# A decoder layer in one kernel: the cross attention's 24 middle steps written out in place of a loop of two, with constant addresses

## What is computed

```python
x = x + gated_slot_attention(layernorm(x))       # 4 heads, a recurrence over the 128 tokens
x = x + cross_attention(layernorm(x), ctx)       # 16 heads of 8
x = x + experts(layernorm(x))                    # 8 experts, top 2, LoRA pairs
```

```python
q = (query @ Wq.T + bq);  k = (key @ Wk.T + bk);  v = (value @ Wv.T + bv)     # heads of 8
scores = einsum(q, k) * 8 ** -0.5 + attn_mask
scores = where(pad, -inf, scores) + spatial_bias + directional_bias           # one array, twice
out = softmax(scores) @ v;  return out @ Wo.T + bo
```

## Time and profile before

| what | value |
|---|---|
| median of 3 runs | 597.54 us (595.57 to 598.49) |
| the profiled execution's own time | 593.18 us |
| its span in the profile | 591.4 us |
| slot attention, alone or in the lead | to about 217 us |
| cross attention, steps 4 to 27 (the loop) | about 242 to 418 us |
| experts | from about 432 us |
| mean granted TensorE clock | 0.987 of full speed |

### The profile page before, as it was taken

One profiled execution on the slowest core, in us unless ns is written; L12 is line 12 of the kernel. 1 busy time (PEld: TensorE's weight loads), 2 busy tenths in 40 slices (PEclk: granted clock), 3 DMA queues, 4 the chain that ended last, 5 costly groups with the idle time before them and its releaser, 6 DMA issues.

```text
span 591.4 us, 17340 instructions
## 1 busy us (share of the span) xinstructions
PE 530.9 (90%) x5328; PEld 408.2 (69%) x5328; DVE 481.9 (81%) x1945; ACT 398.3 (67%) x1033; POOL 355.5 (60%) x362
## 2 busy tenths in 40 slices
PE   4689999999997779999999999999976999999986
PEld 3467677777776547777777777777765778788865
DVE  2578888887877678999999999999988888888862
ACT  2668878878875378988999999999954333333321
POOL 6335555456445898888888888888824433333430
PEclk9899999999999989999999999999989999999999
DMA  6920000000000477888888888888600000000000
GB/s 159 241 37 2 1 1 1 0 0 0 1 1 2 81 130 130 154 154 150 153 153 150 153 151 152 150 154 152 104 2 2 1 19 19 18 18 18 19 18 19
DMA packets 84426, 42.44 MB, mean 72 GB/s; under 512 B 4378, under 2 KB 84132, under 8 KB 84388
## 3 DMA queue, kind: packets, MB, share of 16 engines
q1 hardware_dynamic: 83234, 41.63, 38.5%
q10 hardware_dynamic: 1154, 0.33, 0.2%
HBM read 39.86 MB, written 2.10 MB: 71 GB/s over the span
## 4 chain that ended last, share of the span: by engine, by line
PE 44%; DVE 22%; issue 19%; ACT 5%; POOL 5%; DVEq 1%; POOLq 0%; ACTq 0%
DVE c_P L1044 6%; PE banks L458 5%; PE banks L938 5%; PE banks L925 4%; PE banks L1246 4%; PE banks L891 3%; PE banks L1270 3%; DVE shared L723 3%; PE banks L914 2%; PE banks L449 2%; PE banks L422 2%; PE banks L904 2%; DVE banks L696 2%; DVE shared L702 2%; ACT c_P L972 2%
## 5 line engine op out<-in xcount | busy, mean ns | idle before, releaser
L1138 POOL TENSOR_TENSOR c_bias<-c_fside,c_cm 128x2048 f32<-128x2048 f32 x32 | 146.3, 4571 | 27.3 <-PE banks L891 24.6
L972 ACT ACTIVATE c_P<-c_P,c_min 128x128 f32<-128x128 f32 x512 | 156.6, 391 | 2.4 <-DVE c_min L1044 2.4
L1044 DVE CUSTOM_DVE_ANT_0 c_P<-banks,c_bias 128x128 f32<-128x128 f32 x512 | 116.3, 284 | 5.3 <-PE banks L891 2.3
L925 PE MATMUL banks<-ident,c_P 128*128 128x128 f32 x512 | 74.8, 279 | 6.6 <-DVE shared L1080 5.8
L925 PEld LDWEIGHTS banks<-ident,c_P 128*128 128x128 f32 x512 | 57.9, 142 | 32.9 <-issue 28.4
L1080 DVE COPY shared<-banks 128x512 f32<-128x512 f32 x96 | 65.6, 684 | 0.0
L1246 PE MATMUL banks<-um,lb_s 128*128 128x512 f32 x192 | 55.6, 404 | 2.7 <-ACT shared L1303 1.9
L1482 POOL TENSOR_TENSOR xs<-shared,xs 128x512 fp32r<-128x512 f32 x8 | 10.7, 1334 | 66.5 <-ACT xs L1313 66.5
L1303 ACT ACTIVATE shared<-banks,bi_col 128x512 f32<-128x512 f32 x32 | 22.0, 688 | 38.2 <-PE banks L1246 38.2
L1246 PEld LDWEIGHTS banks<-um,lb_s 128*128 128x128 f32 x192 | 34.2, 188 | 18.9 <-ACT shared L1303 12.5
L1044 DVE DVE_READ_ACCUMULATOR2_ANT c_min<- 128x1 f32 x512 | 42.5, 83 | 0.0
(11 more groups left out here) (195 smaller groups left out, 1295.3 us busy)
## 6 DMA issues: line engine op xcount, KB each, us to landing
c_fside<-in_fside_Bx16xSxS_dram SPq DMA_DIRECT2D x64, 512.0 KB, 7.2
c_ctx<-in_ctx_dram SPq DMA_DIRECT2D x32, 64.0 KB, 5.0
out_dram<-shared SPq DMA_DIRECT2D x8, 256.0 KB, 2.3
X<-in_x_dram SPq DMA_DIRECT2D x3, 512.0 KB, 5.5
kmask_sb<-in_mask_BxS_bf_dram SPq DMA_DIRECT2D x1, 512.0 KB, 7.4
X<-in_x_dram SPq DMA_DIRECT2D x2, 128.0 KB, 3.3
c_P<-in_L_ffn_wi_dram SPq DMA_DIRECT2D x1, 256.0 KB
c_P<-in_L_ffn_lora_B_dram SPq DMA_DIRECT2D x1, 256.0 KB
```

The source lines that it names most:

```text
L925: last = nc.tensor.transpose(bank(2 + i % 2)[:, 128 * j:128 * j + 128], P[:, q, XG * i + j, :], ident[:])
L972: last = nc.scalar.activation(P[:, par, h, :], P[:, par, h, :], ACT.Exp, bias=mn[:, par, h:h + 1], scale=-1.0)
L1044: last = nc.vector.tensor_tensor_reduce(out=P[:, o, h, :], in0=bank(score_banks(n + 1)[i])[:, 128 * j:128 * j + 128], in1=fm[:, o, h, :], ...
L1138: nc.gpsimd.tensor_tensor(fm[:, q, :, :], fs[:, q, :, :], bc(cm[:], XH), ALU.add).then_inc(C["fm"], 1)
```

## The change

The four engines no longer loop over steps 4 to 27: their code holds each of the 24 steps, made by the same function as the steps at both ends, so with constant addresses and constant counts in the waits. The operations, their order on each engine and their buffers are the same. SyncE's loop of loads stays, and so do the loops of the other two stages.

```diff
         def x_loop(engine, step):
-            with engine.Fori(2, B // 2 - 2, 1) as m:
-                step(m, 0, True, True, True, True, True)
-                step(m, 1, True, True, True, True, True)
+            for n in range(4, B - 4):
+                x_peeled(step, n)
```

## The result

The changed kernel takes 588.17 us in the median (586.12 to 590.89, 4 runs) against 597.46 us of before (595.57 to 598.49): a ratio of 0.9864 with a 95% interval of 0.9815 to 0.9913. Its profiled execution took 586.37 us, that of before 593.18, so 6.8 us less at the same mean granted clock of 0.987. The forecast was 590.3 by the medians and 586.0 by the profiled execution.

The account below looks back on a forecast made before the run. VectorE was taken to arrive last in the loop, ScalarE and TensorE together to bind written-out steps. Gains of 5.4, 1.6 and 0.2 us sum to 7.2, off the median 597.54: 590.3 us, 8-in-10 range 586.0 to 595.5.

Parts of the forecast that it names:

- The sum: Cross attention, steps 4 to 27: all 24 go to 7.04 us from a stretch of 176.17, gaining 7.2 us.
- The jump and the address work: VectorE arrives last in the loop; eleven steps with jumps back gain 5.4 us, twelve others 1.6, the first 0.2.
- gain nothing by themselves: TensorE, ScalarE and GpSimd: their register work and jumps hide under waits, so no gain of their own.
- VectorE at 6.94: VectorE's time between additions to the stream in written-out code, claimed as its limit per step, below TensorE's 7.04 us.
- the wait for the queries' copy: Written-out steps: TensorE's wait for ScalarE's copy (L983) before the value product is the limit, 0.1 us each step.
- waits before its sums: GpSimd stands 0.83 and 0.66 us before its sums, so its own register work and jump hide there.
- Fetching: Written-out code needs about 19 and 14 more instruction packets beside the bias loads, costed at nothing; uncovered, 27 us.
- Rival C: Code arrives late and TensorE stands still 1.4 us per packet, 19 times: 20 us slower, 617 us; chance 0.07.
- B: No gain, as bias loads on the busy DMA engines take over: 597.5 us or anything between; chance 0.09.
- Rival A: The jump alone is gained; written-out steps keep a VectorE limit of about 7.11 us: 592.0 us; chance 0.12.
- The time: Whole kernel: the gain of 7.2 us taken off the median of 597.54 gives 590.3 us; off the profiled execution, 586.0.

Follow-up runs that it names:

- TensorE alone: Only TensorE's 24 steps written out, the other engines looping as in the kernel before: 593.04 us by one execution, stretch of the 24 steps 176.19 us.
- three together: TensorE, ScalarE and GpSimd written out, VectorE keeping its loop, against the kernel before: 593.14 us, ratio 0.9935, stretch 175.05 us.
- the loop of four: The kernel before with four steps in the loop body in place of two, on all four engines: 664.93 us, ratio 1.107.
- The four copies: The changed kernel with VectorE's first copy of turned weights (L1080) made in four pieces of 128 columns: 593.03 us, stretch 174.02 us.

## Why the prediction was right, and where it was not

**The sum.** 7.2 us were forecast and 7.0 measured over the stretch. The pattern read from single steps carried it, though the loop is a little less even than my sum has it (its third step lasts 7.77): 7.04 for a written-out step with loads and fetches held for 23 of 24. The number came from that measured step, and not from the account of what bounds it, which was only partly right (below). The 0.35 us of the odd step are not in my sum. The parts ahead of the stretch and behind it kept their lengths to 0.1 us in the profile of 586.37 us, as forecast.

**The jump and the address work.** That VectorE arrived last in the loop was right for 4.6 of the 7.0 us. That the other engines "gain nothing by themselves" was nearly right (0.0 for TensorE alone, 1.1 for three together), but it is not the whole story: once VectorE's loop was gone, 2.3 us more went with the loops of TensorE and GpSimd, by the waits with TensorE's register work and jump, and only then were 7.04 reached. An engine's loop costs what it costs when that engine is the last. How much of the price is the jumps and how much the address work is told in the prediction only by kinds of step (5.4 us in those with a jump, 1.8 in the others); no run separated the two, since the loop of four, made for it, brought a cost of its own.

**VectorE at 6.94.** This step of the reasoning failed. I read 6.94 us from one addition to the stream to the next as what VectorE would allow. But the first of these two additions came late, from a loop step, after 0.32 us of waiting, and the second after 0.21: the 0.1 us between 6.94 and 7.04 is that difference. The round that counts goes through both engines, and can be read from the timelines above: score products at 375.46 (382.49 less 7.03), first score at 376.86, division at 381.51, bias product 0.34 us behind it at 381.85, next score products at 382.49: 1.40 + 4.65 + 0.34 + 0.64 = 7.03 us. The four copies showed that it has no slack. Nor was the limit the wait for the queries' copy alone, as I had it: with that copy made earlier the steps stayed at 7.03 to 7.05.

**GpSimd.** I wrote that it waits before its sums and has room. The wait is part of a round of its own: root (375.36, for 0.55), normalised batch (375.97), mask (376.22), sum (376.59, for 4.58), keys, root. It is 7.03 us from root to root (375.36 to 382.39), and it binds at 7.02 in the two kernels with the bias product moved.

**Fetching.** I costed it at nothing, and but for the odd step, whose cause is open, nothing it was: 18 large packets more against 19 forecast, 15 small ones more against 14, TensorE alone at 176.19 us, bias loads at 90.3% with no wait for a landing. Rival C did not occur, nor B. The sentence that no fetch accompanied the jumps of before was confirmed from the other side by the loop of four, where it did, at 14 us a jump. The Trainium skill, "Runtime: NRT & Kernel Launch", section Instruction fetch mechanics, says just that: a taken branch whose target is outside the current window has to fetch it first. This case agrees on both sides: with VectorE's two steps in the loop no packet of queue 14 moves from 264 to 418 us, with four 26 do.

**Rival A** (the written-out steps stay at 7.11) did not occur in the changed kernel. Steps of 7.10 to 7.20 stood where only VectorE was written out, but a limit of VectorE was not the reason: they went away with TensorE's and GpSimd's loops.

**The time.** Taking the profile's gain off the median gave 590.3 against 588.17. The 2 us between are of the size of what the granted clock between the stages does to one execution, so that the medians come this close is partly luck.

## What to carry to other kernels

When a loop's ends are written out with the same steps, the profile of before already holds the price of the loop: compare single steps inside and outside it, and sum the difference by kinds of step. Don't take the limit of an engine from the time between two of its operations: follow the round through all engines, and expect several rounds of equal length in a tuned pipeline, so that relieving one brings almost nothing. Before making a loop's body longer, look at whether instruction packets move inside the loop; here two steps moved none, four cost 14 us a jump, and no loop at all was the best.

## What the hardware showed unexpectedly

A loop body twice as long made each jump back cost 14 us (246.87 - 176.17 = 70.7 us over five jumps), all of it through VectorE's body, while TensorE's, ScalarE's and GpSimd's bodies of four steps cost nothing. Straight code, in contrast, was fetched beside loads that fill 90.3% of the DMA engines with 23 of 24 steps at 7.03 to 7.05 us.

One step in the written-out code is about 0.35 us longer, at the same place in five profiles of four kernels with the same VectorE program (7.38 or 7.39 us). VectorE's timeline of the changed kernel shows it before the first score:

```profile
383.46 0.28 DVE L1052 BATCH_NORM_STATS2 stats<-X 128x6 f32<-128x128 f32 x1
384.25 0.29 DVE L1044 CUSTOM_DVE_ANT_0 c_P<-banks,c_bias 128x128 f32<-128x128 f32 x1 [0.50 <-PE banks L925]
```

0.50 us of waiting, against 0.15 in other steps. The profile names TensorE's transposes as what ended it, but those came at their usual time. With three more vector instructions in each step two steps are longer instead, elsewhere, by 0.28 and 0.26 us, one of them with VectorE idle for 0.19 us in the midst of its scores and put down to issue. Kernels in which VectorE loops show no such step behind the first pass.

The obvious reading is the border between two fetched pieces of VectorE's code, but the runs speak against its plain form. The two kernels with the bias product moved have the same VectorE program too. There the step at this place lasts 7.24 us (bias product alone) and 7.14 (with the queries earlier), while another, eleven steps earlier, lasts 7.36 and 7.45. In the one of 7.45 us VectorE stands before its division:

```profile
312.35 0.29 DVE L1075 TENSOR_TENSOR shared<-banks,shared 128x128 f32<-128x128 f32 x1 [0.54 <-issue]
```

So the place is not given by VectorE's code alone. And with VectorE alone written out, 12 packets of queue 14 move in the stretch, where the kernel before had 3: some nine pieces are fetched, and one step is 0.2 us longer than its neighbours. An ordinary border costs nothing that can be seen. The cause stays open.
